# A fused transformer step on one core: masks and distances in quarter tiles, residual, GELU counts and input LayerNorm in another order

## The chip, the cores and the metric

One Trainium2 chip, one of its cores. The metric is the time of one execution on the device in microseconds (us); a lower one is better. The kernel is one launch that does six stages one after the other.

## The reference, cut to what matters

The stages work on 16 sequences of 256 tokens with 128 channels, and every stage takes a LayerNorm of `x` as input and adds its result to `x`. Stages 1 and 3 are the same small two-layer model (called ffn below; it takes most of the time), stage 2 is an attention with 16 heads of 8 channels and a distance bias (attn below). Stages 4 to 6 (a mixture of experts, a linear attention, the mixture again) aren't touched by the change.

```python
def _layer(x, wqkv, qs, ksc, wo, lg, lb, w1, b1, w2, b2):      # ffn: two of these per sequence
    h = shift_token(x)
    q, k, v = jnp.split(h @ wqkv, 3, axis=-1)                   # 8 heads of 64
    q, k = l2norm(q) * qs, l2norm(k) * ksc
    q, k = rotary_xpos(q, k)
    o = local_attention(q, k, v)                                # masked to a band of 64 + 64 keys
    x = x + o @ wo                                              # "the residual"
    h = shift_token(x)
    h = (h - mu) / jnp.sqrt(var + 1e-05) * lg + lb
    a, g = jnp.split(h @ w1 + b1, 2, axis=-1)
    return x + (a * gelu(g)) @ w2 + b2
...
mask = (i < j) | (i > j + WINDOW)                               # local_attention
sim = jnp.where(mask, -jnp.finfo(sim.dtype).max, sim)
...
scores = jnp.einsum('bhid,bhjd->bhij', q, k) / scale            # attn
scores = scores + _alibi_bias(...)                              # -slope[h] * |i - j|
```

## The kernel before, in words

Each engine has its own written-out program, and semaphores (`wait_ge`, `then_inc`) tie them together; nothing is scheduled by a planner. In ffn the work is 32 items (two layers times 16 sequences), first the 16 of layer 0, then the 16 of layer 1. Each engine's loop runs over `k`; in step `k` it does the first part of item `k` (`new`: q, k and v projections, rotation, norms), the middle of item `k-1` (`mid`: transposes, scores, softmax, attention) and the last part of item `k-2` (`old`: output projection, residual, LayerNorm, up, GELU, gate, down). While the loop is in layer 0 it also does the LayerNorm of the ffn's input for a sequence ahead (`pre`: `x_mean`, `x_center`, `x_square`, `x_var`, `x_rstd`, and `normed` on POOL, which writes `Y`, from which `split_h` makes the high and low part that `qk` multiplies). Before the change this is the next item's.

The steps that the prediction follows, with lines of the profile of before:

- PE in a step, in this order: turned q and k (L1327), `qk` of the first 128 tokens (L1318 to L1320), `proj` (L1457), `scores` (masks L1377, products L1382), `y_mean` (L1464), `qk` of the other tokens, `y_var`, `v_proj`, `m_T` (L1391, the turned row maxima), `up` (L1475), `x_mean` (L1493), `scores_T` (masks L1402, products L1409 and L1413, in three groups), `down` (L1486), and `attend` (L1438, L1446) with `x_var` (L1498) between its halves.
- DVE: `k_out`, `cosines` (L919), `resid` (L970, the residual), `s_max` (L943, L948), `m_split` (L958, L959), `gated` (L987), `resid2` (L995), `qk_norm` (L936), `o_norm` (L911).
- ACT: copies of q and k (L609, L610), of the projection (`copy_qk`, L589), `gelu` (L638), exponentials.
- POOL: `sines` (L485), `rotated` (L493), `normed` (L500), `split_h` (L510, L512).

A mask is put into PSUM ahead of the score products by a matmul: an identity in bfloat16 as the stationary operand, the mask tiles as the moving one, 128 rows by 128 columns of the array (written 128\*128 in the profile). In the products two matmuls with 64 rows each stand in the two halves of the array (64\*128), and in `attend` four with 32 columns each (128\*32).

In attn, `scores` does in each of eight steps per sequence two heads plainly (for the row maxima, banks 0 and 1, read by DVE L1076) and two turned (for the exponentials, banks 4 and 5, read by ACT L700); the part of the bias that isn't linear comes from 4 matmuls each of a slope matrix by a ramp (L1595, L1602), of 128 columns.

Of the kernel before, what the change touches and what calls it, by code (L numbers as in the profile page):

```python
# [28 lines left out]
P = 128  # L29
# [35 lines left out]

def shape_constants():
# [46 lines left out]
    slope_eye = np.concatenate([-2.0 * m * eye for m in slopes], 1)  # L113
# [4 lines left out]
    parts = dict(rot=rot, masks=np.concatenate([st0, st1, s0, s1], 1), relu=np.concatenate([relu_pf, relu_fp], 1),  # L118
# [9 lines left out]
def build(nc, io, at):  # L128
    ctx = ExitStack()
    with ctx:  # L130
# [37 lines left out]
        masks = sb("masks_bf", [P, 2 * JW], BF16)  # L168
        mst0, mst1 = masks[:, 0:J0W], masks[:, J0W:JW]
        ms0, ms1 = masks[:, JW:JW + P], masks[:, JW + P:2 * JW]  # L170
        sel = sb("m_rows_bf", [P, HEADS, P], BF16)
        tab = sb("rot_tables", [P, DEPTH, 2, TILES, 2, DH])
        relub = sb("relu_bf", [P, 2, P], BF16)
        slopeb = sb("slope_eye_bf", [P, AH, P], BF16)
# [88 lines left out]
        ysum = [sb(f"tile_y_sum{n}", [P, D]) for n in range(2)]  # L263
        yrow = [sb(f"tile_y{n}", [P, D]) for n in range(4)]
# [194 lines left out]
        def _(pool):  # L459
# [17 lines left out]
            def ffn(f):  # L477
# [17 lines left out]
                def normed(s):  # L495
                    n = f * SEQS + s
                    free(pool, f_sum, 2 * (f * ITEMS + s))
# [17 lines left out]
                for k in range(-1, ITEMS):  # L515
# [58 lines left out]
        def _(act):  # L574
# [8 lines left out]
            def ffn(f):  # L583
# [258 lines left out]
        def _(dve):  # L842
# [16 lines left out]
            link(dve.tensor_copy(masks[:, :], part("masks")))  # L859
            link(dve.tensor_copy(relub[:, :, :].rearrange("p a b -> p (a b)"), part("relu")))  # L860
# [41 lines left out]
            def ffn(f):  # L902
# [982 lines left out]
```

## Time and profile before

| | us |
|---|---|
| runs of the kernel (3) | 2479.73, 2481.72, 2485.17; median 2481.72 |
| the profiled execution's own time | 2473.8 |
| its span in the profile | 2471.8 |
| PE busy in the span | 2194.1 (89%) |
| DVE, ACT, POOL busy | 1708.8, 1466.5, 1096.0 |

Engines: PE is the matrix engine's matmuls, PEld its weight loads, DVE the vector engine, ACT the scalar engine, POOL GpSimd. The granted clock of a stretch is a share of 2.4 GHz: 1.00 is 2.4 GHz, 0.5 is 1.2 GHz. The duration of a matmul in a row runs until its result is there, and matmuls follow each other before that: what one occupies is the distance to the start of the next.

### The profile page before, as it was taken

To read this page: it belongs to the slowest core of one execution; us is meant where nothing else is said; L and a number is where in the kernel's file an instruction comes from. 1 tells how busy PE (TensorE), PEld (TensorE's weight loads), DVE (VectorE), ACT (ScalarE), POOL (GpSimd) and SP (SyncE) were. 2 spreads that over 40 slices of the span, in tenths; PEclk is the share of its full clock that TensorE was granted. 3 is DMA by queue.
4 is the path that set the end of the run, shared out by engine and by line. 5 is a ranking of instruction groups with operands and counts; after the bars stand their busy time and mean duration, and the time that the engine had idled before them with its cause. 6 is when DMAs were issued, how large, how long until landed. Compare 5 with 4: busy or idle time off the path is not lost. (4 is left out here: it accounts for less than half of the span.)

```text
span 2471.8 us, 54760 instructions
## 1 busy us (share of the span) xinstructions
PE 2194.1 (89%) x22630; PEld 1635.5 (66%) x22630; DVE 1708.8 (69%) x2815; ACT 1466.5 (59%) x2389; POOL 1096.0 (44%) x800
## 2 busy tenths in 40 slices
PE   2799999999999869999969999999999997697968
PEld 1567767777777656666636666677777774495758
DVE  3677777878878546777737777778888884563556
ACT  0476767667676515556546667677677674363634
POOL 4655555656556110000026565656556550550245
PEclk8799999999999969999979999999999998698979
DMA  7000000069999970000000000000000003121122
GB/s 154 1 2 1 2 2 1 1 78 124 131 146 148 147 85 1 2 2 2 2 1 1 2 2 2 1 2 2 1 2 2 2 1 78 52 66 36 35 75 79
DMA packets 211370, 91.01 MB, mean 37 GB/s; under 512 B 79700, under 2 KB 206721, under 8 KB 210996
## 3 DMA queue, kind: packets, MB, share of 16 engines
q1 hardware_dynamic: 202596, 72.27, 21.8%
q0 software_dynamic: 6080, 11.76, 1.5%
q10 hardware_dynamic: 2448, 3.48, 0.7%
q8 instruction: 181, 2.97, 0.5%
q14 instruction: 65, 0.53, 0.1%
HBM read 24.51 MB, written 63.41 MB: 36 GB/s over the span
## 5 line engine op out<-in xcount | busy, mean ns | idle before, releaser
L485 POOL TENSOR_TENSOR work<-work,rot_tables 128x512 f32<-128x512 f32 x256 | 448.2, 1771 | 423.8 <-ACT work L589 423.8
L493 POOL TENSOR_TENSOR work<-work 128x1024 f32<-128x1024 f32 x128 | 303.5, 2371 | 11.2 <-DVE work L919 1.2
L919 DVE TENSOR_TENSOR work<-work,rot_tables 128x1024 f32<-128x1024 f32 x128 | 164.9, 1288 | 124.9 <-ACT work L589 124.9
L1076 DVE TENSOR_REDUCE small<-psum 128x4 f32<-128x1024 f32 x128 | 156.6, 1224 | 94.7 <-PE psum L1595 94.6
L1318 PE MATMUL psum<-qkv_w_hi,h_hi 128*128 128x512 f32 x384 | 184.5, 481 | 41.4 <-POOL h_lo L512 39.1
L1475 PE MATMUL psum<-centered,ffn_w 128*128 128x256 f32 x768 | 191.4, 401 | 6.1 <-DVE centered L980 2.9
L936 DVE TENSOR_TENSOR work<-work,small 128x1024 f32<-128x1024 f32 x128 | 160.3, 1254 | 48.9 <-ACT small L603 47.0
L700 ACT ACTIVATE work<-psum 128x1024 f32<-128x1024 f32 x128 | 131.2, 1025 | 101.1 <-PE psum L1602 101.1
L1413 PE MATMUL psum<-work 64*128 64x128 f32 (+1 forms) x2048 | 178.9, 304 | 0.0
L500 POOL TENSOR_TENSOR y_all<-centered,squared 64x256 f32<-64x256 f32 x64 | 48.6, 760 | 290.6 <-ACT squared L649 288.1
L1475 PEld LDWEIGHTS psum<-centered,ffn_w 128*128 128x128 f32 x768 | 146.3, 197 | 36.5 <-DVE centered L980 17.7
L1446 PE MATMUL psum<-work,v 128*32 128x192 f32 (+1 forms) x4096 | 162.6, 299 | 0.0
L589 ACT ACTIVATE work<-psum 128x1024 f32<-128x1024 f32 x128 | 130.3, 1018 | 50.2 <-PE psum L1320 50.2
L617 ACT ACTIVATE work<-psum 128x768 f32<-128x768 f32 (+1 forms) x192 | 154.5, 873 | 1.6 <-PE psum L1413 1.4
L925 DVE TENSOR_REDUCE small<-qk_squares 128x16 f32<-128x1024 f32 x128 | 154.8, 1209 | 0.4 <-ACT qk_squares L594 0.4
L1320 PE MATMUL psum<-qkv_w_hi,h_lo 128*128 128x512 f32 x384 | 154.7, 403 | 0.0
L1319 PE MATMUL psum<-qkv_w_lo,h_hi 128*128 128x512 f32 x384 | 154.5, 402 | 0.0
L554 POOL DMA_INDIRECT h_area<-rows,position x64 | 62.3, 974 | 199.5 <-DVE position L1158 173.0
L758 ACT ACTIVATE qk_squares<-psum,work 128x128 f32<-128x128 f32 x312 | 89.2, 369 | 92.4 <-PE psum L1736 92.4
L1413 PEld LDWEIGHTS psum<-work 64*128 64x128 f32 x2048 | 142.4, 188 | 0.0
L536 POOL CAST h_hi<-centered 128x256 fp32r<-128x256 f32 x16 | 6.3, 397 | 301.5 <-DVE centered L1059 301.5
L594 ACT ACTIVATE qk_squares<-work 128x1024 f32<-128x1024 f32 x128 | 135.4, 1058 | 2.0
(283 smaller groups left out, 5530.3 us busy)
## 6 DMA issues: line engine op xcount, KB each, us to landing
h_area<-mean_weights SPq DMA_DIRECT2D x24, 2048.0 KB, 24.8
tile_x<-h_area SPq DMA_DIRECT2D x39, 128.5 KB, 2.1
stage<-in_consts ACTq DMA_DIRECT2D x1, 3009.0 KB, 12.4
tile_x<-h_area SPq DMA_DIRECT2D x39, 64.5 KB, 1.8
work<-in_x SPq DMA_DIRECT2D x4, 512.0 KB, 27.6
expert_w<-in_ew SPq DMA_DIRECT2D x1, 2048.0 KB, 8.5
expert_w<-in_ew SPq DMA_DIRECT2D x8, 256.0 KB, 6.8
work<-y_tokens SPq DMA_DIRECT2D x4, 512.0 KB, 6.0
```

What stands on the lines that cost most here:

```text
L485: last = pool.tensor_tensor(b[:, :, :, o_], a[:, :, :, i_], tab[:, l, 1, t, :, o_].unsqueeze(2).to_broadcast([P, 2, HEADS, 32]), ALU.mult)
L493: pool.tensor_tensor(rC[:, t, :], rC[:, t, :], rB[:, t, :], ALU.add).then_inc(f_sum, 1)
L617: act.activation(PT[:, hs, a:a + w].rearrange("p (h b) j -> p b h j", b=2), PS[:, bs, 0:m * w].rearrange("p b (h j) -> p b h j", h=m), ACT ...
L919: dve.tensor_tensor(g(rC[:, t, :]), g(rA[:, t, :]), tab[:, l, 0, t, :, :].unsqueeze(2).to_broadcast([P, 2, HEADS, DH]), ALU.mult)\
L925: dve.tensor_reduce(sm[0][:, 16 * t:16 * t + 16], sq[:, t, :].rearrange("p (g d) -> p g d", d=DH), AX, ALU.add).then_inc(f_ss, 1)
L936: dve.tensor_tensor(c_, c_, sm[0][:, 96 + 16 * t:112 + 16 * t].unsqueeze(2).to_broadcast([P, 16, DH]), ALU.mult).then_inc(f_nrm, 1)
L1076: dve.tensor_reduce(dst, PS[:, 0:2, :].rearrange("p b (t j) -> p b t j", t=TILES), AX, ALU.max, negate=True).then_inc(a_smax, 1)
L1318: pe.matmul(out, hi, w_hi, start=True, stop=False)
L1320: return pe.matmul(out, lo, w_hi, start=False, stop=True)
L1413: last = pe.matmul(PS[:, bs[h % 2], o:o + w], kT[rows_(h), h // 2, j * P:(j + 1) * P], qT[rows_(h), h // 2, i0:i0 + w], start=False, stop= ...
L1446: last = pe.matmul(PS[32 * q:32 * q + 32, (4, 2)[a], z * T + lo:z * T + hi], V[i % 2][:, j, d:d + 32], PT[:, 4 * a + q, src:src + hi - lo] ...
L1475: last = pe.matmul(PS[:, b, o:o + T], fw[:, l, o2 + c * P:o2 + (c + 1) * P], ycen[:, :], start=True, stop=True)
```

## The change

It does five things.

1. The mask matmuls of ffn (`bands`) are each split over four 64 by 64 quarters of the array: two row halves (each of which writes a bank, as in the products) times two column halves (each of which writes 64 partitions). The identity becomes a 64 by 64 one, and the mask tiles lie in SBUF so that every quarter finds its 64 rows on its own partitions. Two matmuls become four.
2. The distance matmuls of attn (`distances`) likewise: 4 quarters with a 64 by 64 slope matrix and 2 times 128 columns in place of 4 whole ones of 128 columns.
3. DVE does `resid` of item `k-2` ahead of `cosines(k, 0)`.
4. Each of the three GELUs counts for itself in `f_g`, and each of the three `gated` waits for its own.
5. The input's LayerNorm runs two items ahead: all ffn loops begin at `k = -2`, and on POOL `split_h` of the next item stands ahead of `normed` of the one after it.

The tables of constants change their layout with 1 and 2, and two small sets of tiles of the mixture of experts move into a part of `work1` that is free then, to make room.

```diff
+            def bands(bs, n, w, m):
+                for half in range(2):
+                    for r, b in enumerate(bs):
+                        k_, o_ = slice(64 * r, 64 * r + 64), slice(64 * half, 64 * half + 64)
+                        pe.matmul(PS[o_, b, 0:n * w], eyeb[k_, k_],
+                                  masks[k_, half, m].unsqueeze(1).to_broadcast([64, n, w]),
+                                  start=True, stop=False, skip_group_check=True)
...
                     for bs, hs, w, _, _, m in groups:
-                        n = len(hs) // 2
-                        for b in bs:
-                            pe.matmul(PS[:, b, 0:n * w], eyeb[:, :], m.unsqueeze(1).to_broadcast([P, n, w]),
-                                      start=True, stop=False, skip_group_check=True)
+                        bands(bs, len(hs) // 2, w, m)
...
+                def distances(b0, pair, first):
+                    for half in range(2):
+                        for r in range(2):
+                            k_, o_ = slice(64 * r, 64 * r + 64), slice(64 * half, 64 * half + 64)
+                            blocks = PS[o_, b0 + r, :].rearrange("p (a c) -> p a c", c=P)[:, 0::3, :]
+                            last = pe.matmul(blocks, slopeb[k_, pair, :], relub[k_, half, first:first + 2, :],
+                                             start=False, stop=True, skip_group_check=True)
+                    return last
...
                     if plain:
-                        for b in range(2):
-                            for t in range(TILES):
-                                a = t * T + t * P
-                                last = pe.matmul(PS[:, b, a:a + P], slopeb[:, 2 * p + b, :], relub[:, 1 - t, :],
-                                                 start=False, stop=True, skip_group_check=True)
-                        last.then_inc(a_s, 1)
+                        distances(0, p, 1).then_inc(a_s, 1)
...
                     if new:
-                        cosines(i, 0)
-                    if old:
                         resid(i - 2)
+                    if new:
+                        cosines(i, 0)
```

The last piece reads in the source as a move: `if old: resid(i - 2)` now stands ahead of `if new: cosines(i, 0)`. GELU, gate and the LayerNorm:

```diff
                     for c, b, o in ((0, 4, 0), (1, 4, T), (2, 0, 0)):
-                        last = act.activation(G[:, c, :], PS[:, b, o:o + T], ACT.Gelu, bias=b1[:, l, HC + c:HC + c + 1])
-                    last.then_inc(f_g, 1)
+                        act.activation(G[:, c, :], PS[:, b, o:o + T], ACT.Gelu, bias=b1[:, l, HC + c:HC + c + 1])\
+                            .then_inc(f_g, 1)
...
-                    dve.wait_ge(f_g, i + 1)
                     for c, b, o in ((0, 1, 0), (1, 1, T), (2, 0, T)):
+                        dve.wait_ge(f_g, HC * i + c + 1)
...
-                for k in range(-1, ITEMS + 2):
-                    i, n = f * ITEMS + k, f * SEQS + k + 1
-                    new, mid, old, pre = 0 <= k < ITEMS, 0 <= k - 1 < ITEMS, 0 <= k - 2, k + 1 < SEQS
+                for k in range(-2, ITEMS + 2):
+                    i, n = f * ITEMS + k, f * SEQS + k + 2
+                    new, mid, old, pre = 0 <= k < ITEMS, 0 <= k - 1 < ITEMS, 0 <= k - 2, k + 2 < SEQS
...
-                    if k + 1 < SEQS:
-                        normed(k + 1)
-                    if k + 1 < ITEMS:
+                    if 0 <= k + 1 < ITEMS:
                         split_h(i + 1)
+                    if k + 2 < SEQS:
+                        normed(k + 2)
```

What this does to the order of instructions, at three places. First PE, in a layer 0 step, from `x_mean` to `down`; `masks_bf` are the mask tiles, `m_rows_bf` and `work` belong to the products. Before:

```order
L1493 MATMUL psum<-x_all,mean_weights 128x256 [waits ffn_mT_sb,pre_rstd]
L1402 MATMUL psum<-masks_bf,eye_bf 128x384 [waits ffn_qk_sb]
L1402 MATMUL psum<-masks_bf,eye_bf 128x384
L1402 MATMUL psum<-masks_bf,eye_bf 128x512 [waits ffn_v_sb]
L1402 MATMUL psum<-masks_bf,eye_bf 128x512
L1409 MATMUL psum<-mT,m_rows_bf 128x192 [waits ffn_mT_sb]
```

and now, up to the third group:

```order
L1500 MATMUL psum<-x_all,mean_weights 128x256 [waits ffn_mT_sb,pre_rstd]
L1339 MATMUL psum<-masks_bf,eye_bf 64x384 [waits ffn_qk_sb]
L1339 MATMUL psum<-masks_bf,eye_bf 64x384 x3
L1339 MATMUL psum<-masks_bf,eye_bf 64x512 [waits ffn_v_sb]
L1339 MATMUL psum<-masks_bf,eye_bf 64x512 x3
L1416 MATMUL psum<-mT,m_rows_bf 128x192 [waits ffn_mT_sb]
L1416 MATMUL psum<-mT,m_rows_bf 128x192 x3
L1420 MATMUL psum<-work 128x192 x4
L1416 MATMUL psum<-mT,m_rows_bf 128x128 x8
L1420 MATMUL psum<-work 128x128 x8
L1339 MATMUL psum<-masks_bf,eye_bf 64x384 [waits ffn_gated]
```

Each pair of mask matmuls is four of half the partitions with the same columns; the order and the waits are the same. Second DVE, at the turn of a step, from the copy of k to the first row maxima. Before:

```order
L906 CAST kT_bf<-work 128x1024 [waits chain]
L919 TENSOR_TENSOR work<-work,rot_tables 128x1024 [waits ffn_qT,ffn_qk_sb]
L970 TENSOR_TENSOR y_all<-y_all,psum 64x256 [waits ffn_proj]
L970 TENSOR_TENSOR y_all<-y_all,psum 64x256
L943 TENSOR_REDUCE small<-psum 128x4 [waits ffn_s]
```

and now:

```order
L911 CAST kT_bf<-work 128x1024 [waits chain]
L975 TENSOR_TENSOR y_all<-y_all,psum 64x256 [waits ffn_proj]
L975 TENSOR_TENSOR y_all<-y_all,psum 64x256
L924 TENSOR_TENSOR work<-work,rot_tables 128x1024 [waits ffn_qT,ffn_qk_sb]
L948 TENSOR_REDUCE small<-psum 128x4 [waits ffn_s]
```

The two halves of the residual, with their wait for `proj`, have moved ahead of the multiplication by the cosines. Third POOL, the end of a layer 0 step. Before:

```order
L493 TENSOR_TENSOR work<-work 128x1024 [waits ffn_cos,ffn_sin]
L500 TENSOR_TENSOR y_all<-centered,squared 64x256 [waits pre_rstd,ffn_rot]
L500 TENSOR_TENSOR y_all<-centered,squared 64x256 [waits ffn_y0]
L510 CAST h_hi<-y_all 128x256 [waits ffn_qk,ffn_y0]
L512 TENSOR_TENSOR h_lo<-y_all,h_hi 128x256 [waits ffn_h_split]
```

and now:

```order
L498 TENSOR_TENSOR work<-work 128x1024 [waits ffn_cos,ffn_sin]
L515 CAST h_hi<-y_all 128x256 [waits ffn_qk,ffn_y0]
L517 TENSOR_TENSOR h_lo<-y_all,h_hi 128x256 [waits ffn_h_split]
L505 TENSOR_TENSOR y_all<-centered,squared 64x256 [waits pre_rstd,ffn_rot]
L505 TENSOR_TENSOR y_all<-centered,squared 64x256 [waits ffn_y0]
```

The split of the next item's input no longer stands behind the wait for `pre_rstd`, which ACT gives at the end of its step.

## Rows read from the trace of the kernel before

**Rows 1.** The page's first part: busy us, share of the span, instructions.

```profile
PE 2194.1 (89%) x22630; PEld 1635.5 (66%) x22630; DVE 1708.8 (69%) x2815; ACT 1466.5 (59%) x2389; POOL 1096.0 (44%) x800
```

**Rows 2.** Windows, busy us by engine: a layer 0 item, a layer 1 item, an attn sequence.

```profile
319.05:343.87 24.82, 23.76 (x260) 17.39 (x259) 18.75 (x29) 17.43 (x28) 14.25 (x10) 1.00 0.01 2
676.56:699.99 23.43, 22.98 (x254) 16.86 (x255) 19.17 (x30) 16.23 (x25) 13.73 (x8) 1.00 1.16 135
1053.54:1074.90 21.36, 20.19 (x257) 14.57 (x253) 15.76 (x20) 12.66 (x17) 1.12 (x2) 1.00 0.01 2
```

**Rows 3.** Timeline of PE in that layer 1 item: start, us, line.

```profile
679.58 0.92 PE L1402 MATMUL psum<-masks_bf,eye_bf 128*128 128x384 bf16 x4
680.43 0.34 PE L1409 MATMUL psum<-mT,m_rows_bf 64*128 64x192 bf16 x4
...
682.84 0.50 PE L1402 MATMUL psum<-masks_bf,eye_bf 128*128 128x384 bf16 x2 [0.22 <-DVE gated L987]
683.27 0.34 PE L1409 MATMUL psum<-mT,m_rows_bf 64*128 64x192 bf16 x4
...
686.28 1.27 PE L1446 MATMUL psum<-work,v 128*32 128x192 f32 x32
...
692.11 1.89 PE L1457 MATMUL psum<-o_T,ffn_w 128*128 128x256 f32 x8
693.84 1.25 PE L1377 MATMUL psum<-masks_bf,eye_bf 128*128 128x512 bf16 x6
695.01 0.73 PE L1382 MATMUL psum<-kT_bf,qT_bf 64*128 64x128 bf16 x16
```

**Rows 4.** Timeline of DVE in the same item.

```profile
681.52 1.27 DVE L987 SCALAR_TENSOR_TENSOR gated<-psum,b,gelu 128x256 f32<-128x256 f32 x3 [0.71 <-ACT gelu L638]
...
693.61 1.22 DVE L919 TENSOR_TENSOR work<-work,rot_tables 128x1024 f32<-128x1024 f32 x1 [1.18 <-ACT work L589]
694.76 0.84 DVE L970 TENSOR_TENSOR y_all<-y_all,psum 64x256 f32<-64x256 f32 x2
695.63 1.29 DVE L943 TENSOR_REDUCE small<-psum 128x4 f32<-128x512 f32 x2
```

**Rows 5.** Timeline of ACT in the same item.

```profile
680.20 1.21 ACT L638 ACTIVATE gelu<-psum,b 128x256 f32<-128x256 f32 x3
...
692.55 1.03 ACT L589 ACTIVATE work<-psum 128x1024 f32<-128x1024 f32 x1
```

**Rows 6.** Single lines, the last two in that attn sequence: ns, least, median and most.

```profile
L1486 PE MATMUL psum<-gated,ffn_w x384: 379/379/483, 128.0 to 2077.7; 128*128 128x256 f32 x192
...
L1614 PE MATMUL psum<-work x68: 379/379/403, 1053.2 to 1074.6; 128*32 128x256 f32 x68
...
L1595 PE MATMUL psum<-relu_bf,slope_eye_bf x32: 219/219/230, 1054.6 to 1073.5; 128*128 128x128 bf16 x32
```

**Rows 7.** Waits of PE from 169.9 to 418.5 us, ten layer 0 items.

```profile
PE psum L1318 <- POOL h_lo L512: 10.6, 10, 1.1
```

**Rows 8.** Timeline of PE, POOL and DVE in a layer 0 item.

```profile
334.74 0.50 PE L1318 MATMUL psum<-qkv_w_hi,h_hi 128*128 128x512 f32 x1 [1.01 <-POOL h_lo L512]
...
336.24 1.89 PE L1457 MATMUL psum<-o_T,ffn_w 128*128 128x256 f32 x8
...
331.93 1.53 POOL L500 TENSOR_TENSOR y_all<-centered,squared 64x256 f32<-64x256 f32 x2 [6.35 <-ACT squared L649]
...
339.58 1.29 DVE L943 TENSOR_REDUCE small<-psum 128x4 f32<-128x512 f32 x2
```

**Rows 9.** Timeline of PE in attn, from one step's scores to the next.

```profile
1065.73 0.38 PE L1585 MATMUL psum<-k_slots,q_slots 32*128 32x256 f32 x2 [0.20 <-ACT work L700]
...
1066.16 0.40 PE L1595 MATMUL psum<-relu_bf,slope_eye_bf 128*128 128x128 bf16 x4
1066.40 0.39 PE L1602 MATMUL psum<-relu_bf,slope_eye_bf 128*128 128x128 bf16 x4
...
1068.28 0.38 PE L1585 MATMUL psum<-k_slots,q_slots 32*128 32x256 f32 x2 [0.36 <-DVE small L1076]
```

More of the change, by code:

```diff
@@ L112, in shape_constants @@
         lo_k[r + 16:r + 24] = -1.0
-    slope_eye = np.concatenate([-2.0 * m * eye for m in slopes], 1)
+    slope_eye = np.concatenate([np.concatenate([-2.0 * m * eye[0:64, 0:64] for m in slopes[r::2]], 1) for r in range(2)], 0)
     block = (p // LDH == f // LDH).astype(np.float32)
@@ L262, in build @@
         gT = [sqs[:, 512 * n:512 * n + 512].rearrange("p (c t) -> p c t", c=EC) for n in range(3)]
-        ysum = [sb(f"tile_y_sum{n}", [P, D]) for n in range(2)]
-        yrow = [sb(f"tile_y{n}", [P, D]) for n in range(4)]
+        ysum = [work[1][:, 4608 + D * n:4608 + D * (n + 1)] for n in range(2)]
+        yrow = [work[1][:, 4864 + D * n:4864 + D * (n + 1)] for n in range(4)]
         o1, o2, o3 = 0, 4 * P, 4 * P + 2 * HC * P
@@ L513, in split_h @@
                         .then_inc(f_h, 1)
-                for k in range(-1, ITEMS):
+                for k in range(-2, ITEMS):
                     i = f * ITEMS + k
@@ L1008, in x_center @@
                     dve.tensor_tensor(ocen[:, :], X[:, n % SEQS, :], PS[:, 7, T:2 * T], ALU.subtract).then_inc(o_cen, 1)
-                for k in range(-1, ITEMS + 2):
-                    i, n = f * ITEMS + k, f * SEQS + k + 1
-                    new, mid, old, pre = 0 <= k < ITEMS, 0 <= k - 1 < ITEMS, 0 <= k - 2, k + 1 < SEQS
+                for k in range(-2, ITEMS + 2):
+                    i, n = f * ITEMS + k, f * SEQS + k + 2
+                    new, mid, old, pre = 0 <= k < ITEMS, 0 <= k - 1 < ITEMS, 0 <= k - 2, k + 2 < SEQS
                     if old:
@@ L1397, in scores_T, with masked @@
                               ((0, 1), range(4, 8), J0W, 0, 0, mst0))
-                    def bands(bs, hs, w, j, i0, m):
-                        q = len(hs) // 2
-                        for b in bs:
-                            pe.matmul(PS[:, b, 0:q * w], eyeb[:, :], m.unsqueeze(1).to_broadcast([P, q, w]),
-                                      start=True, stop=False, skip_group_check=True)
+                    def masked(bs, hs, w, j, i0, m):
+                        bands(bs, len(hs) // 2, w, m)
                     def products(bs, hs, w, j, i0, m):
@@ L1501, in ffn @@
                 free(pe, x_done, SEQS * 2 * f)
-                for k in range(-1, ITEMS + 2):
-                    i, n = f * ITEMS + k, f * SEQS + k + 1
-                    new, mid, old, pre = 0 <= k < ITEMS, 0 <= k - 1 < ITEMS, 0 <= k - 2, k + 1 < SEQS
+                for k in range(-2, ITEMS + 2):
+                    i, n = f * ITEMS + k, f * SEQS + k + 2
+                    new, mid, old, pre = 0 <= k < ITEMS, 0 <= k - 1 < ITEMS, 0 <= k - 2, k + 2 < SEQS
                     if mid:
@@ L1591, in scores @@
                     if plain:
-                        for b in range(2):
-                            for t in range(TILES):
-                                a = t * T + t * P
-                                last = pe.matmul(PS[:, b, a:a + P], slopeb[:, 2 * p + b, :], relub[:, 1 - t, :],
-                                                 start=False, stop=True, skip_group_check=True)
-                        last.then_inc(a_s, 1)
-                    if turned:
-                        for b in range(2):
-                            for t in range(TILES):
-                                a = t * T + t * P
-                                last = pe.matmul(PS[:, 4 + b, a:a + P], slopeb[:, 2 * r + b, :], relub[:, t, :],
-                                                 start=False, stop=True, skip_group_check=True)
-                        last.then_inc(a_st, 1)
+                        distances(0, p, 1).then_inc(a_s, 1)
+                    if turned:
+                        distances(4, r, 0).then_inc(a_st, 1)
                 def attend(w):
```

39 lines of the change are left out of this document (21 added, 18 removed).

## The prediction, made blind

> **What bounds the kernel now.** First the page: PE is busy 89% of the span, DVE 69% [rows 1], so PE looks like the bound, and less PE work like a gain of the same size. That has to be read in the single item. The windows give a layer 0 item of ffn 24.82 us, a layer 1 item 23.43 and an attn sequence 21.36, all at a granted clock of 1.00 [rows 2]; two ffn with 16 items of each layer and 16 sequences are some 1885 us of 2471.8.
>
> Then the waits. In layer 0 PE stands still once per item, 1.06 us on average, at the first `qk` matmul, for POOL's low half of the input [rows 7]; that row begins with POOL having waited 6.35 us for ACT's reciprocal root [rows 8]. In layer 1 no such wait exists, and yet PE isn't free. Its third group of masks starts 0.22 us late, for `gated` [rows 3]. Otherwise the item is a closed loop over three engines: PE `up`, `scores_T`, `down`, DVE `resid2`, `qk_norm` and `o_norm`, PE turned q and k, ACT copies and `copy_qk` (692.55), DVE `cosines` (693.61), `resid` (694.76), `s_max` (695.63), and from there DVE in one piece to `m_split` and PE's `m_T` at 699.99, the end of the window [rows 2 to 5]. DVE's `cosines` waits 1.18 us for ACT and nothing behind it waits [rows 4]. So from 692.55 to 699.99 it is the DVE chain that sets the time, and PE work saved there (the masks of `scores`, at 693.84) is no gain. What is saved between `m_T` and the turned q and k is one.
>
> **The masks.** A price for a wave of four quarters isn't in the trace: no form is 64\*64. What is: six whole matmuls of 2560 columns go from 693.84 to 695.01, 1.17 us, which is 2560 / 2.4 GHz = 1.07 and 0.10 for the switch to the next form; the 64\*128 products behind them, 2560 columns too, have their last start and result within 0.73 us, so the two row halves run together. The four columns of 128\*32 do too: 32 matmuls of 160 columns on average in float32, which takes two cycles a column (`proj`'s eight of 256 columns: 1.89 less 0.17 is 0.22 each), would need 4.27 us one by one and take 1.27 [rows 3]. I take a wave of four quarters as one pass of its columns: 384 are 0.16 us, 512 are 0.22. Behind a switch the first weight load shows: 0.104 us for 128 columns in float32 (483 against 379), 0.024 for 32 (403 against 379), 0.011 for 128 in bfloat16 (230 against 219) [rows 6]. For 64 columns I take 0.05, between the first two; bounds 0.01 and 0.10.
>
> The Trainium skill ("TensorEngine Tiling (Array Packing)", Restrictions and Gotchas) says that column tiling turns off the fast weight load; by it the 0.011 can't be had and 0.05 is right. It is small either way (3 x 0.04 us per item).
>
> Groups one and two of `scores_T`: now 679.58 to 680.43, 0.85 us. After: switch 0.10, load 0.05, 0.16 + 0.22, switch 0.10, sum 0.63: **-0.22 us** per item. Group three in layer 1: PE idles 0.22 us up to 682.84, so the last result before it came at 682.62, and a result comes 0.17 behind the last column (219 ns for 128 columns, which occupy 53) [rows 3, 6]; the array was free at 682.45. The products of group three begin at 683.27: 0.82 us. After: 0.10 + 0.05 + 0.16 + 0.10 = 0.41, if nobody waits: **-0.41**. In layer 0 it doesn't wait now, so it is 0.53 (two waves of 0.16 and a switch at either end) to 0.41: **-0.12**.
>
> Nobody waits, because of the count per GELU: the three start from 680.20, 0.37 apart, DVE was ready 0.71 before 681.52 [rows 4, 5], so the gates run from 680.81 and end at about 682.1 in place of 682.8; PE needs them at 682.3. Without this count the masks would be ready earlier and the wait longer. The counts themselves cost nothing: an increment rides on an instruction.
>
> These prices rest on a switch being needed between 64\*64 and 64\*128. The same page (Tiling Modes) says that any change of the mode drains the engine; the trace agrees for the forms it has, with 0.10 us each. If a change of the columns alone is free, three switches fall away in the loop, 0.29 us per item: the first rival.
>
> **The residual first.** It waits for `proj`: PE's last result at 692.11 + 1.89 = 694.00, DVE starts at 694.03, its two halves take 0.87, then the cosines 1.15 (693.61 to 694.76), so `s_max` starts at 696.05 and not 695.63: **+0.42** in layer 1 [rows 3, 4]. In layer 0: 336.24 + 1.89 = 338.13, by the same steps 340.18 against 339.58: **+0.60** [rows 8]. Queued behind it are the cosines, for which POOL's `rotated` waits, and `s_max`, for which PE's second `qk` half waits. PE comes to that half about when `s_max` is done now; with the masks of `scores` at 0.79 in place of 1.17 us (entry 0.10, load 0.05, waves 0.22 + 0.16 + 0.16, exit 0.10) it comes 0.4 earlier and `s_max` is 0.4 later, so PE will stand there 0.8 to 0.9 us. What the move buys, an earlier `y_mean`, lies beside that.
>
> **Input two items ahead.** POOL's split no longer waits for ACT: **-1.01** in layer 0 [rows 8], the whole wait, as the split then follows POOL's `rotated` directly, before POOL's idle 6.35 us. `normed` still waits those on POOL; behind it are the next item's `sines`, which need `copy_qk` and so the `qk` matmuls of 334.74. The new first step of each ffn adds one LayerNorm chain ahead of item 0, beside POOL's 1.5 + 1.1 us for item 0 [rows 8]; at the other end one item less carries the two means, 4 x 0.22 us and a switch each way, 1.2. Taken as **-1.2** per ffn, bounds -1.2 and +2.
>
> **Sum for ffn.** Layer 0: -1.01 - 0.22 - 0.12 + 0.60 = -0.75 us, 32 items, -24.0. Layer 1: -0.22 - 0.41 + 0.42 = -0.21, 32 items, -6.7. Ends -2.4. Together -33.1.
>
> **The distances.** Now eight of 128 columns, 1066.16 to about 1066.62, 0.46 us; after, 0.05 and two waves of 256 columns, 0.27: -0.19 per step, 128 steps, -24 at most. But PE waits in these steps, for ACT at 1065.73 and for DVE at 1068.28 [rows 9]. A wait for ACT ends 0.19 earlier, one for DVE (the plain half: result after 0.40 now, 0.05 + 0.11 + 0.17 later) only 0.07. And where a whole-array matmul stood right behind the turned ones (`m_T`, the mean), a switch of 0.10 with its load comes in. I take about 0.11 in four of the eight steps and nothing in the others: -0.45 per sequence, **-7.2** (bounds -24 and +6). Fewer constants to fetch (by 384 of its columns): -1, bounds -1 and 0.
>
> **Total** -33.1 - 7.2 - 1 = -41.3 us. The profiled execution itself took 2473.8, so 2432.5; the median of the runs stands 7.9 above it, 2440.4. I say 2441.
>
> **The rivals.**
>
> No switch between quarter and half-row forms: 64 x 0.29 = -18.6, 2422. For it: both have 64 rows. Against: every change of form that the trace has costs 0.10. 0.15.
>
> The residual costs nothing, because something that I don't see holds `s_max` back: 32 x 1.02 = -32.6 more, 2408. Against it: DVE doesn't pause between `resid` and `s_max` [rows 4]. 0.07.
>
> The gain is largely given back: the wait for `s_max` or for DVE in attn is longer than reckoned, by 0.3 to 0.5 us an item; 2455 to 2476. 0.11.
>
> **Slower**: the four quarters don't run together. If only the row halves do, every wave takes double: 0.54 us per item, +34.6, attn gives +4 in place of -7.2, sum 2487, slower by 0.2%. One after the other: 1.62 us per item more, +104, and 0.45 per step of attn, +58, 2610. It decides from about 1.9 passes per wave on. For it: the trace has row pairs and column fours, never both at once. Against: neither shows a limit shared with the other. 0.08.
>
> The granted clock drops in attn, where PE gets idler: 20.19 of 21.36 us are at 1.00 now [rows 2]; each sequence at 1.2 GHz, where columns take twice the time, would cost up to 18 us more, so from two or three on the gain is gone. 0.04.
>
> **How the numbers follow.** 0.55 for the forecast (2428 to 2455), the rest as given. A measurement here can tell about 0.2%, 5 us. Faster: 0.55 + 0.15 + 0.07 + 0.09 = 0.86; same 0.05; slower 0.09. The range of 2414 to 2477 leaves out the full form of the second rival and the slow ones.
>
> **What would show it.** A step from one 64\*64 wave to the next of 0.16 and 0.22 us, with starts a few ns apart; 0.10 between forms. Layer 0 items of 24.1 and layer 1 items of 23.2 us. No wait of PE for `h_lo` or `gated`; a new wait of `qk` for `s_max` near 0.9 us, DVE idle ahead of `resid`, not of `cosines`. Attn sequences of 20.9. It is wrong if waves take two passes, if items of layer 1 go under 22.9 or if the new wait isn't there.

## The result

| | us |
|---|---|
| before, median of 20 runs | 2480.12 (2471.45 to 2486.92) |
| after, median of 20 runs | 2476.33 (2456.78 to 2482.07) |
| ratio after to before | 0.9966, 95% interval 0.995 to 0.9982 |
| the profiled execution of after | 2476.3, its span 2474.5 |

A gain of 0.34%, where 1.6% was forecast (2441, range 2414 to 2477). The range just holds the time, by its width and not by the sum: its upper end was set by a rival at another price. The direction and most steps were right; one step, the residual, was far off, and it ate nearly all of the rest.

Page of after, first part, for [rows 1]:

```profile
PE 2133.3 (86%) x23398; PEld 1572.0 (64%) x23398; DVE 1762.1 (71%) x2815; ACT 1464.2 (59%) x2389; POOL 1056.6 (43%) x800
```

PE has 61 us less to do and the kernel is hardly shorter. DVE runs the same 2815 instructions and is busy 53 us longer, POOL the same 800 and 39 us less. Nobody gave DVE work: the same instructions last longer. That is the first thing to follow.

Windows of after, columns as in [rows 2]: a layer 0 item, a layer 1 item, an attn sequence:

```profile
333.18:356.99 23.81, 22.94 (x271) 16.82 (x271) 19.14 (x29) 17.33 (x28) 14.34 (x10) 1.00 0.01 2
1786.06:1810.13 24.07, 22.02 (x268) 16.28 (x267) 20.22 (x30) 16.24 (x25) 12.64 (x8) 1.00 0.01 2
1056.74:1077.48 20.74, 18.82 (x256) 12.12 (x252) 15.67 (x20) 12.58 (x17) 1.12 (x2) 1.00 0.01 2
```

Against [rows 2] a layer 0 item is 1.01 us shorter, a sequence 0.62, and a layer 1 item 0.64 **longer**, with DVE busy 20.22 us in it where it was 19.17, and PE 22.02 where it was 22.98.

Timeline of after in that layer 1 item, masks of `scores_T` and the gate:

```profile
1789.10 0.57 PE L1339 MATMUL psum<-masks_bf,eye_bf 64*64 64x384 bf16 x8
1789.60 0.34 PE L1416 MATMUL psum<-mT,m_rows_bf 64*128 64x192 bf16 x4
...
1790.47 1.27 DVE L992 SCALAR_TENSOR_TENSOR gated<-psum,b,gelu 128x256 f32<-128x256 f32 x3
...
1791.79 0.36 PE L1339 MATMUL psum<-masks_bf,eye_bf 64*64 64x384 bf16 x4
1792.08 0.34 PE L1416 MATMUL psum<-mT,m_rows_bf 64*128 64x192 bf16 x4
```

The first two groups take 0.50 us up to the products where they took 0.85 [rows 3]; the third takes 0.29, where it took 0.43 and stood 0.22 ahead of that. Up to here the item runs as forecast. The same item at its turn, DVE, POOL and PE, for [rows 4]:

```profile
1802.47 2.50 POOL L490 TENSOR_TENSOR work<-work,rot_tables 128x512 f32<-128x512 f32 x2 [7.73 <-ACT work L594]
1802.84 0.85 DVE L975 TENSOR_TENSOR y_all<-y_all,psum 64x256 f32<-64x256 f32 x2 [1.59 <-PE psum L1464]
1803.73 2.32 DVE L924 TENSOR_TENSOR work<-work,rot_tables 128x1024 f32<-128x1024 f32 x1
1806.08 1.29 DVE L948 TENSOR_REDUCE small<-psum 128x4 f32<-128x512 f32 x2
...
1807.42 0.50 PE L1323 MATMUL psum<-qkv_w_hi,h_hi 128*128 128x512 f32 x1 [1.97 <-DVE small L948]
```

`cosines` takes 2.32 us where it took 1.22, with no wait in front of it. Before the change it was POOL that paid. Timeline of POOL before the change, the row that belongs beside [rows 4]:

```profile
693.66 3.54 POOL L485 TENSOR_TENSOR work<-work,rot_tables 128x512 f32<-128x512 f32 x2 [8.60 <-ACT work L589]
```

Both engines were released by the same copy of ACT (693.58); DVE started at 693.61, POOL at 693.66, and POOL's two `sines` took 3.54 us (2.30 and 1.27). Now POOL starts them at 1802.47, while DVE is at the residual, and needs 2.50 for both; its second one starts at 1802.47 + 1.24 = 1803.71, DVE's `cosines` at 1803.73. The one that starts 0.02 us later takes 1.1 us longer. In layer 0 of the same kernel it falls the other way:

```profile
350.49 3.55 POOL L490 TENSOR_TENSOR work<-work,rot_tables 128x512 f32<-128x512 f32 x2 [3.29 <-ACT work L594]
350.80 0.85 DVE L975 TENSOR_TENSOR y_all<-y_all,psum 64x256 f32<-64x256 f32 x2 [1.60 <-PE psum L1464]
351.68 1.23 DVE L924 TENSOR_TENSOR work<-work,rot_tables 128x1024 f32<-128x1024 f32 x1
...
354.28 0.50 PE L1323 MATMUL psum<-qkv_w_hi,h_hi 128*128 128x512 f32 x1 [0.87 <-DVE small L948]
```

POOL's second `sines` starts at 351.71; DVE is at work by 351.68 and keeps its 1.23 us, and POOL's takes 2.33.

The Trainium skill ("SBUF — State Buffer", Who interferes with whom) states that a VectorE instruction with two SBUF inputs contends with a GpSimd instruction that reads SBUF, and that "Issue order, not op shape, decides who blocks." The traces agree in the direction; in size a blocked operation ends 0.15 us sooner than a full exclusion would make it (POOL's second `sines` ends 1.24 us into the 2.32, and 1.24 + 1.23 = 2.47).

### The profile page after: what moved, and what is told of

Read it like the earlier page. It is cut to its first block and busy times, and to the rows that moved or that the text cites. A ratio compares the mean times of both kernels' runs of the same rounds, so it can differ in the third digit from the quotient of the medians.

```text
span 2474.5 us, 56322 instructions
## 1 busy us (share of the span) xinstructions
PE 2133.3 (86%) x23398; PEld 1572.0 (64%) x23398; DVE 1762.1 (71%) x2815; ACT 1464.2 (59%) x2389; POOL 1056.6 (43%) x800
## 5 line engine op out<-in xcount | busy, mean ns | idle before, releaser
L490 POOL TENSOR_TENSOR work<-work,rot_tables 128x512 f32<-128x512 f32 x256 | 411.0, 1626 | 483.8 <-ACT work L594 483.8
L1323 PE MATMUL psum<-qkv_w_hi,h_hi 128*128 128x512 f32 x384 | 189.6, 494 | 90.0 <-DVE small L948 87.7
L924 DVE TENSOR_TENSOR work<-work,rot_tables 128x1024 f32<-128x1024 f32 x128 | 211.0, 1648 | 19.2 <-ACT work L594 17.4
L941 DVE TENSOR_TENSOR work<-work,small 128x1024 f32<-128x1024 f32 x128 | 166.9, 1306 | 76.3 <-ACT small L608 72.1
L632 ACT ACTIVATE squared<-centered 128x256 f32<-128x256 f32 x64 | 26.8, 419 | 244.9 <-DVE centered L981 244.9
L1323 PEld LDWEIGHTS psum<-qkv_w_hi,h_hi 128*128 128x128 f32 x384 | 74.7, 195 | 138.5 <-DVE small L948 114.2
```

Source lines behind the costliest of these rows:

```text
L490: last = pool.tensor_tensor(b[:, :, :, o_], a[:, :, :, i_], tab[:, l, 1, t, :, o_].unsqueeze(2).to_broadcast([P, 2, HEADS, 32]), ALU.mult)
L924: dve.tensor_tensor(g(rC[:, t, :]), g(rA[:, t, :]), tab[:, l, 0, t, :, :].unsqueeze(2).to_broadcast([P, 2, HEADS, DH]), ALU.mult)\
L941: dve.tensor_tensor(c_, c_, sm[0][:, 96 + 16 * t:112 + 16 * t].unsqueeze(2).to_broadcast([P, 16, DH]), ALU.mult).then_inc(f_nrm, 1)
L1323: pe.matmul(out, hi, w_hi, start=True, stop=False)
```

## Where the time went, stretch by stretch

Layer 0 is the time from the first `m_T` of an ffn to its 17th, layer 1 from there to its last, both ffn added; cosines are those of the first 128 tokens, in most items. All of it is read from one execution each, the ratio from all runs.

| kernel | median us | ratio (95%) | layer 0 | layer 1 | cosines, layer 0 / 1 |
|---|---|---|---|---|---|
| before | 2480 | 1 | 785.1 | 700.2 | 1.23 / 1.23 |
| after | 2476.3 | 0.9966 (0.995 to 0.9982) | 762.2 | 733.6 | 1.23 / 2.32 |
| e4 quarters alone | 2462.0 | 0.993 (0.9908 to 0.9952) | 780.7 | 699.4 | 1.23 / 1.23 |
| e8 quarters, counts | 2437.1 | 0.9817 (0.9797 to 0.9837) | 772.6 | 686.1 | 1.23 / 1.23 |
| e7 two ahead alone | 2458.7 | 0.9898 (0.9868 to 0.9928) | 760.8 | 702.7 | 1.23 / 1.23 |
| e1 after, residual back | 2405.7 | 0.9696 (0.9674 to 0.9719) | 747.6 | 687.5 | 1.23 / 1.23 |
| e2 residual alone | 2565.9 | 1.034 (1.0306 to 1.0373) | 828.0 | 744.4 | 2.06 / 2.32 |
| e3 sines wait | 2432.0 | 0.9807 (0.9783 to 0.9831) | 759.7 | 694.3 | 1.23 / 1.23 |
| e11 POOL memset more | 2431.7 | 0.9802 (0.9763 to 0.9842) | 755.4 | 688.5 | 1.22 / 1.22 |
| e6 DVE memset more | 2413.9 | 0.9723 (0.9686 to 0.976) | 745.6 | 685.2 | 1.16 / 1.16 |
| e9 memset, waited for | 2470.5 | 0.9957 (0.9937 to 0.9978) | 782.1 | 708.1 | 2.27 / 2.21 |
| e5 writes later | 2405.4 | 0.9686 (0.9665 to 0.9707) | 745.5 | 677.6 | 1.23 / 1.23 |

## The experiments

**The residual back (e1).** Part 3 alone is undone.

```diff
-                    if old:
-                        resid(i - 2)
                     if new:
                         cosines(i, 0)
+                    if old:
+                        resid(i - 2)
```

> Only part 3 is undone: the residual stands behind the first cosines again, as before the change. Theory A (the move makes DVE's cosines start 21 ns behind POOL's second sines, and the engine that starts second on these two operands waits for the first, 2.32 us in place of 1.23; on top comes the residual's own 0.87 us ahead of the row maxima): the cosines of layer 1 are 1.23 us again, items of layer 1 fall from 24.06 to about 22.9 us, items of layer 0 from 23.8 to about 23.3, the whole to about 2420 us. Theory B (the move costs only its 0.42 and 0.60 us per item, and the rest of the slow-down of layer 1 comes from the quarters or from the LayerNorm two items ahead): layer 1 stays at 23.6 or above, layer 0 falls to 23.2, the whole is about 2442 us.

2405.66 us, 3.0% under before. Timeline of it, the turn of a layer 1 item:

```profile
1755.68 1.22 DVE L924 TENSOR_TENSOR work<-work,rot_tables 128x1024 f32<-128x1024 f32 x1 [1.19 <-ACT work L594]
1755.73 3.53 POOL L490 TENSOR_TENSOR work<-work,rot_tables 128x512 f32<-128x512 f32 x2 [7.92 <-ACT work L594]
1756.83 0.85 DVE L975 TENSOR_TENSOR y_all<-y_all,psum 64x256 f32<-64x256 f32 x2
...
1757.72 0.70 PE L1471 MATMUL psum<-y_all,mean_weights 128*128 128x256 f32 x2 [0.33 <-DVE y_all L975]
```

and two of its windows, layer 0 and layer 1:

```profile
332.46:356.03 23.57, 23.16 (x270) 16.81 (x271) 19.11 (x29) 17.33 (x28) 14.22 (x10) 1.00 0.01 2
1739.31:1762.04 22.73, 22.18 (x266) 16.28 (x267) 19.14 (x30) 16.22 (x25) 13.71 (x8) 1.00 0.01 2
```

DVE is first again (1755.68 against 1755.73), and the layer 1 item is 1.34 us shorter. Theory A stands, and more came than its 2420: the two layers fell by 14.6 and 46.1 us between the profiled executions (2476.3 and 2418.05), and the other four runs of this kernel, 2400 to 2408, are shorter than its profiled one. PE now waits 0.33 us for the residual, ahead of `y_mean`; that wait is what the move takes away, and all that the rows show of its worth.

**The residual alone (e2)**, on the kernel before, with the same edit the other way round.

> The kernel before with part 3 alone: the residual ahead of the first cosines. Theory A (cosines lose against POOL's second sines): the cosines of layer 1 take about 2.3 us, items of layer 1 go from 23.43 to 24.5 to 24.9 us, items of layer 0 from 24.86 to 25.4, the whole to 2530 to 2545 us. Theory B (only the residual's own time is added): layer 1 at 23.85, layer 0 at 25.46, the whole at about 2513 us.

2565.89 us, 3.4% slower. Timeline of it, a layer 0 and a layer 1 item:

```profile
375.54 2.49 POOL L485 TENSOR_TENSOR work<-work,rot_tables 128x512 f32<-128x512 f32 x2 [2.85 <-ACT work L589]
377.05 2.06 DVE L919 TENSOR_TENSOR work<-work,rot_tables 128x1024 f32<-128x1024 f32 x1
...
1883.67 2.49 POOL L485 TENSOR_TENSOR work<-work,rot_tables 128x512 f32<-128x512 f32 x2 [8.60 <-ACT work L589]
1884.93 2.31 DVE L919 TENSOR_TENSOR work<-work,rot_tables 128x1024 f32<-128x1024 f32 x1
```

Here DVE loses in both layers. In layer 0 it starts 0.28 us behind POOL's second `sines` and takes 2.06, in layer 1 0.02 behind and takes 2.31: the loser's end hangs on the winner's end, which speaks for waiting and not for a slower rate. Theory A again, beyond its figure: it had left out that layer 0 could lose too. An item of layer 0 takes 26.2 us (+1.4), of layer 1 24.93 (+1.5). That is the prediction's 0.60 and 0.42 and the 0.83 and 1.09 that the cosines grow by: 1.43 and 1.51.

**POOL's second half waits (e3)** for DVE's cosines, in layer 1 of the changed kernel.

```diff
                     for h in range(2):
+                        if h == 1 and t == 0 and l == 1:
+                            pool.wait_ge(f_cos, 2 * i + t + 1)
```

> The changed kernel with one wait more: in layer 1 POOL's second half of the sines of the first 128 tokens waits until DVE's cosines of the same tokens are done, so that the two can't run side by side. Theory A (it is POOL's operation, started 21 ns earlier, that holds DVE up): cosines of layer 1 1.23 us in place of 2.32, items of layer 1 from 24.06 to about 23.1 us, POOL's sum at most 0.2 us later, the whole at 2444 us. Theory B (the cosines are slow for another reason, or their length isn't on the path): no change, or an item longer by what POOL waits, 24.1 to 24.5 us, the whole at 2476 to 2490 us.

2432.01 us, theory A, with 23.04 us for an item of layer 1. A wait more on POOL is worth 44 us. Timeline of it, layer 1:

```profile
1773.70 1.27 POOL L492 TENSOR_TENSOR work<-work,rot_tables 128x512 f32<-128x512 f32 x1 [7.80 <-ACT work L596]
...
1774.96 1.23 DVE L926 TENSOR_TENSOR work<-work,rot_tables 128x1024 f32<-128x1024 f32 x1
...
1776.26 1.26 POOL L492 TENSOR_TENSOR work<-work,rot_tables 128x512 f32<-128x512 f32 x1 [1.30 <-DVE work L926]
...
1777.56 0.50 PE L1325 MATMUL psum<-qkv_w_hi,h_hi 128*128 128x512 f32 x1 [0.87 <-DVE small L950]
```

Alone each operation has its 1.23 and 1.27 us, and PE's new wait is 0.87, the 0.8 to 0.9 of the prediction. Against the kernel with the residual back this prices the move without the conflict: 23.80 against 23.57 in layer 0, 0.2 us an item, and 23.04 against 22.73 in layer 1, 0.3. In layer 1 POOL's wait is in it too; with the memset on POOL in its place (e11 below) the item is 22.96, so the move alone is 0.2 to 0.3 there.

**A memset ahead of the cosines (e6)**, on the kernel with the residual back.

```diff
                     free(dve, f_qT, i)
+                    if t == 0:
+                        dve.memset(scrap[:, :], 0.0)
                     dve.tensor_tensor(g(rC[:, t, :]), g(rA[:, t, :]),
```

> The changed kernel with part 3 undone, and a memset of 64 columns on DVE between the wait for the copy of q and k and the first cosines, some 0.1 us of work. Without it DVE starts the cosines 45 ns ahead of POOL's first sines and takes 1.23 us, and POOL pays with 2.3. Theory A (whoever starts first holds the other up): DVE now starts behind POOL, the cosines of the first 128 tokens take 2.3 us or more in every item, and an item gets 1.0 to 1.2 us longer, 64 to 77 us in all: the whole at 2465 to 2485 us for 6 us of work. Theory B (DVE's cosines were slow in the changed kernel for what stands ahead of them, not for the order of the starts): the cosines stay at 1.23 us, an item gets 0.1 us longer, the whole at 2412 us.

A miss: 2413.92 us and items as without it. Timeline of it:

```profile
1756.14 0.11 DVE L926 MEMSET scrap<- 128x64 f32 x1 [1.23 <-ACT work L595]
1756.15 3.54 POOL L491 TENSOR_TENSOR work<-work,rot_tables 128x512 f32<-128x512 f32 x2 [7.92 <-ACT work L595]
1756.17 1.16 DVE L927 TENSOR_TENSOR work<-work,rot_tables 128x1024 f32<-128x1024 f32 x1
```

The memset takes 0.11 us, but the cosines start 0.03 behind its start, so they weren't put off as meant. In that row they even stand 0.02 behind POOL's start, and yet POOL pays; in layer 0 they are ahead of it (349.18 against 349.22). Either an operation of DVE that follows without a pause goes on with what the one before it held, or a start in a row isn't quite the moment of the decision; this run doesn't tell the two apart.

**The same memset, waited for (e9)**: `link(dve.memset(scrap[:, :], 0.0))`.

> The changed kernel with part 3 undone, and ahead of the first cosines the same memset of 64 columns as in the run before, but the cosines now wait until it is done. In that run the memset (112 ns) started 66 ns ahead of POOL's sines and the cosines followed 29 ns behind the memset's start, so DVE was first after all and the cosines took 1.16 us. Now the cosines start some 0.17 us behind the memset's start, after POOL's first sines. Theory A (the order of the two starts decides): the cosines of the first 128 tokens take about 2.3 us in both layers, POOL's first sines 1.27 in place of 2.24 to 2.30, items get 0.9 to 1.2 us longer, the whole is at 2465 to 2485 us against 2405.7. Theory B (the order of the starts does not decide): the cosines stay at 1.2 us, an item is 0.15 us longer, the whole at 2415 us.

2470.46 us, 64.8 more than with the residual back. Timeline of it, a layer 0 item:

```profile
361.25 0.11 DVE L926 MEMSET scrap<- 128x64 f32 x1 [1.23 <-ACT work L595]
361.31 3.46 POOL L491 TENSOR_TENSOR work<-work,rot_tables 128x512 f32<-128x512 f32 x2 [3.30 <-ACT work L595]
361.39 2.27 DVE L927 TENSOR_TENSOR work<-work,rot_tables 128x1024 f32<-128x1024 f32 x1
```

0.14 us of delay costs 1.04 us per item in layer 0 and 0.97 in layer 1. No residual was moved here, so it is the order of the starts. Theory A, with one part not foreseen: POOL's second `sines` paid as well (3.46 for both).

**A memset on POOL (e11)** between its two halves, in layer 1, on the changed kernel as it is.

```diff
+                        if h == 1 and t == 0 and l == 1:
+                            pool.memset(scrap[:, :], 0.0)
```

> The changed kernel as it is, with a memset of 64 columns on POOL between the two halves of the sines of the first 128 tokens, in layer 1 only: pure extra work. In the changed kernel DVE's cosines start there 15 to 29 ns behind POOL's second sines and take 2.32 us. Theory A (the order of the two starts decides): POOL's second half now starts behind DVE, the cosines take 1.23 us in layer 1, items there fall from 24.07 to 23.0 to 23.1 us, the whole is at about 2432 us, as with the wait for the cosines, though the kernel only got an instruction more. Theory B (the wait in the earlier run helped for another reason): the cosines stay at 2.3 us, layer 1 at 24.07 or above, the whole at 2476 us or above.

2431.68 us. Timeline of it:

```profile
1767.85 0.14 POOL L491 MEMSET scrap<- 128x64 f32 x1
1767.90 1.22 DVE L927 TENSOR_TENSOR work<-work,rot_tables 128x1024 f32<-128x1024 f32 x1
1767.95 2.30 POOL L493 TENSOR_TENSOR work<-work,rot_tables 128x512 f32<-128x512 f32 x1
```

Theory A. An instruction that computes nothing of use makes the changed kernel 45 us faster: DVE now starts 0.05 ahead of POOL, has its 1.22, and POOL, which has time, takes 2.30. With the run before it the order of the two starts is shown to decide from both sides; what the memset without a wait (e6) left open, which moment counts as the start, stays open.

**Quarters alone (e4)**, parts 1 and 2, and **quarters with the counts (e8)**, 1, 2 and 4, the rest as before:

> The kernel before with parts 1 and 2 alone (mask and distance matmuls in quarters). Theory A (the quarters give what their steps say, and don't touch the cosines): layer 0 at about 24.6, layer 1 at about 23.3, a sequence of attn at 20.7 as in the changed kernel, the whole at about 2458 us. Theory B (the quarters are what makes layer 1 slow, by shifting PE against the others): layer 1 at 23.8 to 24.1, the whole at 2475 us or more.

> The kernel before with parts 1, 2 and 4: quarters, and a count for each GELU. With the quarters alone layer 1 stood at 23.29 us. Theory A (the third group of masks waits for the gates, and the counts take this wait away, as the sum of the prediction says): layer 1 at 22.75 to 22.9 us as in the changed kernel with part 3 undone, layer 0 unchanged at 24.7, the whole at about 2448 us against 2462.0. Theory B (the counts give nothing, and the rest of layer 1's gain comes with the LayerNorm two items ahead): layer 1 at 23.3 us, the whole at 2462 us.

Theory A in both (2461.96 and 2437.14 us), except that the counts weren't expected to touch layer 0, nor to give this much. Items of layer 0 24.70 and 24.45 us, of layer 1 23.29 and 22.75. Waits of PE in the whole of the first, which the second has no more:

```profile
PE psum L1339 <- DVE gated L992: 16.5, 34, 0.8
```

Without the counts the quarters only turn the saved time into this wait (7.9 us in 34 times before); with them 25 us come free. The counts are the larger half of the gain.

**Two ahead alone (e7)**, part 5: the head of all loops, `normed`, `split_h` and PE's waits as in the change.

> The kernel before with part 5 alone (LayerNorm of the input two items ahead). Theory A (it takes away PE's wait of 1.06 us for the low half of the input in layer 0, and DVE's first scaling by the norms grows from 1.23 to 1.53 us beside POOL's split, since the two overlap now): layer 0 from 24.86 to about 24.0 us an item, layer 1 unchanged at 23.43, the whole at about 2453 us. Theory B (in the changed kernel layer 0 got shorter by the quarters only): layer 0 stays at 24.8 us, the whole is unchanged.

2458.70 us, layer 0 at 23.97 us an item (-0.87), layer 1 at 23.43. Theory A, but for its aside: the first scaling by the norms stays at 1.23 us here. It is 1.53 in the changed kernel and in the one with the residual back, where DVE comes to it while POOL is in `split_h`; `resid2` behind it waits for `down` there in any case, so it costs nothing seen.

**The large writes later (e5)**: SP waits for the end of the first ffn ahead of the loop over the h area, on the kernel with the residual back.

```diff
             sp.wait_ge(id_ready, 2)
+            sp.wait_ge(x_done, SEQS)
             for n in range(2):
```

> The changed kernel with part 3 undone, and the 16 large writes of the h area (24 transfers of up to 2 MB, which run beside layer 1 of the first ffn, about 560 to 900 us) held back until the first ffn has ended. In the kernel without this edit PE stands 2.4 to 2.6 us at four places there, in the middle of its own instructions and waiting for nothing that the profile shows, and the 15 steps of layer 1 take 348.7 us in the first ffn and 338.8 in the second; in the kernel before the change both take 350. Theory A (PE's instructions come late while those transfers run): layer 1 of the first ffn falls to 339 to 340 us, and attn, whose items are then beside the transfers, gains at most a part of it: the whole at 2396 to 2404 us against 2405.7. Theory B (the stalls are a matter of the place in the program): layer 1 of the first ffn stays at 348 us, no change of the whole.

Waits of PE in that kernel from 905 to 1290 us (attn, where the writes are now), of those that end by nothing in the profile the ones that the kernel without this edit has not got:

```profile
PE psum L1583 <- issue: 3.6, 3, 1.7
PE psum L1621 <- issue: 3.2, 1, 3.2
PE psum L1574 <- issue: 3.0, 1, 3.0
```

Layer 1 of the first ffn fell from 348.7 to 338.7 us, as theory A says, and equals that of the second (338.9). But the stalls went with the writes and came back in attn, so that the median is the same, 2405.44: attn and the entry to the second ffn, from the first ffn's last `m_T` to the second's first, took 479.6 us in place of 456.9. In the steady part of attn the granted clock was 0.5 for 16.6 us of this execution, and for 0.6 at most in every other kernel, so not all of it is the stalls themselves. The profiled execution was the longest of its five (2435.6, the others 2402.7 to 2406.7), so what attn pays in the others isn't known.

## Why the prediction was wrong

**What bounds the kernel.** The closed loop over three engines, with DVE in one piece from the turn to `m_split`, was right, and it is why the error was dear: 1.1 us on DVE at the turn came out in full in the item.

**Masks.** Four quarters in one pass, a switch of 0.10 between 64\*64 and 64\*128: right. The four of a wave start 0.003 us apart, the next wave 0.19 behind the first (384 columns, 0.16), the products 0.32 behind that one (512 columns, 0.21, and 0.10). With the counts 0.54 us per item of layer 1 from e4 to e8 and 0.68 in all against a forecast of 0.63; layer 0 0.39 against 0.34. The gate of the item shown ends at 1790.47 + 1.27 = 1791.74 and the masks start at 1791.79: PE waits next to nothing for it. Of the rivals, no switch and quarters one after the other (or in pairs) are out by these rows, the free residual by e3. The lower clock is out where the rival put it, in the sequences of attn (1.00 in the window), but it came elsewhere, as told below.

**Two ahead.** -1.01 forecast, -0.87 measured alone, and 0.88 from e8 to e1. PE waits for `h_lo` no more. The term was 0.14 too large per item, and it was counted for 32 items where two of the sixteen steps of each ffn had no LayerNorm ahead to wait for even before (they took 23.1 us): over the whole of layer 0 it gave 24.3 us (785.1 to 760.8) and not 32.3.

**Attn.** -0.45 a sequence forecast, 0.62 measured [rows 2]. The steady part, from the third `v_proj` to the last, fell from 276.5 to 268.3 us. The stretch from there to the second ffn's first `m_T` grew from 81.2 to 88.4 in the profile of after, and stood at 80.2 to 89.5 in the others, whatever their edit. It goes with the granted clock, 0.81 in it before and 0.67 after: where it took up to 84.9 us, 31 to 41 of them were at 1.2 GHz, and where it took 86.3 or more, 51 to 65. What sets the clock off there is open.

**The residual first: the step that failed.** "Its two halves take 0.87, then the cosines 1.15 (693.61 to 694.76), so `s_max` starts at 696.05 and not 695.63: +0.42". It took the length of `cosines` as a property of the instruction, and it is one of its neighbour. Without the conflict the move costs 0.3 us in layer 1 and 0.2 in layer 0 (e3 against e1), less than 0.42 and 0.60, and the 0.33 us that PE waits for `y_mean` go away with it; the forecast had put that gain beside the path. That the one explains the other is argued, but it fits the kernel before, where PE has next to no such wait in most items: there the move cost 1.36 - 0.83 = 0.53 in layer 0 and 1.50 - 1.09 = 0.41 in layer 1 (e2), near the forecast. With it layer 1 pays 1.03 us more (24.07 against 23.04). So layer 1 is -0.68 + 0.30 + 1.03 = +0.65 (with POOL's wait counted to the move) and not -0.21, layer 0 is -1.27 + 0.24 = -1.03 and not -0.75. Over 32 items each: +20.8 in place of -6.7, and -33.0 in place of -24.0. The sums over whole layers of the profiled executions are +33.4 for layer 1 and -22.9 for layer 0 against before, more on the side of the loss. In layer 0 the gain of 1.03 came in twelve or thirteen steps of sixteen only; the last ones, with no LayerNorm ahead in them, took 23.1 us before and take 23.8 to 24.9 now. In layer 1 six of the fifteen steps in the first ffn take 25.1 to 27.4 us and three in the second 25.1 to 25.2, by the stalls and the clock told of below.

The rival "the gain is largely given back" (2455 to 2476, by a longer wait for `s_max`) named the place and the total. Its price, 0.3 to 0.5 us in every item, was not what happened: nothing more in layer 0, 1.03 in layer 1.

The trace of before held the warning: POOL's `sines` of one shape took 2.30 and 1.27 us, and the long one lay beside `cosines`. Moving `cosines` by 0.87 us moved it onto the second one.

**"Wrong if the new wait isn't there."** It is there, 87.7 us in 61 times over the whole of after, up to 2.0; the forecast's 0.8 to 0.9 holds in layer 0 alone (0.87). The waits name `s_max`; the culprit is one instruction further up and waits for nothing that the profile shows, because a blocked operation counts as busy.

**Not in the forecast at all.** Before, layer 1 took 350.3 and 349.9 us in the two ffn. After it is 371.6 and 362.0, with the residual back 348.7 and 338.8: some 10 us more in the first. Waits of PE in after from 554 to 903 us:

```profile
PE psum L1392 <- issue: 2.4, 2, 1.7
PE psum L1325 <- issue: 2.1, 1, 2.1
PE psum L1332 <- issue: 1.5, 1, 1.5
```

There PE stands in the middle of its own instructions, beside the 24 writes of up to 2 MB into the h area. The kernel before has no such row in that stretch; every other kernel here with the writes in place has some, 2 to 8 us in all, the one with two ahead alone too (3.9) and the one with the residual alone (4.2), so it isn't the 768 additional matmuls of the quarters. That the stalls follow the writes is shown by e5.

That it is PE's instructions that come late can be read from the transfers of the DMA queue for instructions. The trace of after has 187 of 16 KiB on one such queue and 48035 recorded instructions of PE, one transfer for every 257. The three long stalls end at 639.15, 663.80 and 844.74 us, each 1.6 to 1.7 behind the end of one of these transfers (637.54, 662.13, 843.11). In all twelve traces together PE stands 36 times for 0.6 us or more without a wait beside the writes, apart from a few gaps at either end of attn that recur in every kernel. All 36 stand at the same place of a block of 256 instructions of PE, the 193rd or 194th, and each ends 1.0 to 2.5 us behind such a transfer. In after the transfers took 1.6 us beside the writes and 1.1 elsewhere (medians). The kernel before has one of the 36, 0.97 us at 833.20, which the view of waits puts down to ACT. The Trainium skill ("Runtime: NRT & Kernel Launch", Instruction fetch mechanics) says that the fetch runs ahead sequentially and is mostly hidden, apart from branches; no branch stands at these places, and here up to 3.2 us of it show.

After such a pause of PE the granted clock at times falls to 1.2 GHz for a few us. Timeline of PE in after, and two windows, the second in the second ffn, where no large write runs:

```profile
639.15 0.79 PE L1325 MATMUL psum<-qkv_w_hi,h_lo 128*128 128x512 f32 x1 [2.08 <-issue]
639.74 3.13 PE L1464 MATMUL psum<-o_T,ffn_w 128*128 128x256 f32 x8
...
622.28:649.10 26.82, 23.78 (x267) 17.29 (x267) 19.13 (x30) 16.34 (x25) 12.75 (x8) 0.94 1.20 97
1882.30:1907.36 25.06, 23.01 (x267) 16.85 (x266) 21.22 (x31) 16.90 (x25) 12.91 (x9) 0.96 0.00 1
```

`proj` takes 3.13 us where it took 1.89 [rows 3]. In the second window PE has no stall; it waits 1.97 us for `s_max`, up to 1903.67, and from 1905.2 to 1908.6 the clock is at 1.2 GHz. Most steps have the same wait and no fall of the clock. So the wait that the residual brought has a second price at times, about 1 us in each of three of the fifteen steps there. Layer 1 of after has 16.3 and 6.9 us at 1.2 GHz in the two ffn, that of before none.

The best kernel is the change without part 3, at 0.9696 of before (0.9674 to 0.9719), with terms that were all in the forecast: -41.3 less its 32 x 1.02 for the residual is -73.9, and 2480 - 2405.7 is 74. That the two agree so well is in part luck. The profiled executions differ by 56 us (2473.8 and 2418.05), with 37.5 us in layer 0 where the terms give 43.2, and 12.7 in layer 1 where they give 20.2.

## What to carry to other kernels

Before an instruction on DVE with two SBUF inputs is moved, look what POOL does at its new place and who will start first; a twin of the same shape with two lengths in the trace marks such a pair. Then price the move with the long duration as well, and put the conflict on the engine that has time: a wait or one small instruction on POOL was worth 45 us here. A move that ends a wait of 0.33 us isn't worth 0.87 us ahead of the work that bounds the loop, so time the parts of a change apart: four of these five gave 3.0% together, and the fifth took 2.8 points of it back.

## What the hardware showed that was not expected

- Two starts that the rows show 0.02 us apart go with 1.1 us per item, one way or the other: 0.14 us of delay on DVE made a kernel 64.8 us slower, 0.14 us on POOL made one 44.7 us faster.
- The loser's row shows no wait: `cosines` reads as 2.32 us of work. It ends 0.15 us sooner than the two one after the other.
- An instruction with one input in PSUM and one in SBUF is left alone: the residual's halves took 0.42 us beside POOL's `sines` (after) and beside nothing of it alike (0.41 to 0.43 in all 128).
- Quarters of 64 by 64 run four at a time, with 0.10 us for the change to the 64 by 128 form.
- PE stood up to 3.2 us in straight code beside large DMA writes, each time 1.0 to 2.5 us behind the landing of a 16 KiB transfer of its instructions.
- After PE had stood still for about 2 us the granted clock fell to 1.2 GHz for a few us, in some of the steps and not in all.
